# An attention loop in another order, its hand-over to the feed-forward layer a block sooner, and a norm moved from VectorE to ScalarE

## The reference

```python
x = x + attn_a(layernorm(x))   # 2 heads of 64, rotary positions on half of each head, softmax over 256 keys
x = x + ffn(layernorm(x))      # 128 -> 512, gate; 512 -> 512, gelu; 512 -> 512, gelu; 512 -> 128
x = x + attn_b(layernorm(x))   # 16 heads of 8, causal softmax
x = x + ffn(layernorm(x))      # the same weights again
```

## Time and profile before

| | |
|---|---|
| median of 3 runs | 768.71 us (766.55 to 768.84) |
| the profiled execution's own time | 768.21 us |
| its span in the profile | 766.4 us |
| TensorE busy | 685.7 us, 89% |
| VectorE, ScalarE, GpSimd busy | 484.8, 454.9 and 431.0 us |
| granted TensorE clock, mean | 0.977 |

### The profile page before, as it was taken

How to read it: one execution, slowest core, us unless ns; L and a number is a source line. 1 busy time by engine, 2 the same in 40 slices (tenths; PEclk the granted TensorE clock), 3 DMA queues, 4 the chain that set the end, 5 groups by cost and what they waited for, 6 DMA issues and landing times.

```text
span 766.4 us, 13977 instructions
## 1 busy us (share of the span) xinstructions
PE 685.7 (89%) x4706; PEld 472.0 (62%) x4706; DVE 484.8 (63%) x957; ACT 454.9 (59%) x801; POOL 431.0 (56%) x444
## 2 busy tenths in 40 slices
PE   3789896799999999999999999999878899999996
PEld 1455555477787777665555555555445777777784
DVE  6668885567555586456767767766658356675510
ACT  2677774555665565445656566666665555556663
POOL 4455441377867776433444544543555677777763
PEclk9999998899999999999999999999999999999998
DMA  6110320000000003531645654645111000000000
GB/s 182 39 38 20 62 27 2 0 1 1 0 1 0 0 0 99 177 111 43 209 147 177 239 169 156 229 140 180 57 63 41 16 15 15 14 0 15 15 15 27
DMA packets 33028, 52.47 MB, mean 68 GB/s; under 512 B 4560, under 2 KB 9680, under 8 KB 32976
## 3 DMA queue, kind: packets, MB, share of 16 engines
q1 hardware_dynamic: 32784, 51.53, 21.3%
q10 hardware_dynamic: 192, 0.26, 0.1%
HBM read 27.15 MB, written 24.38 MB: 67 GB/s over the span
## 4 chain that ended last, share of the span: by engine, by line
PE 48%; DVE 13%; POOL 13%; issue 12%; ACT 8%; DMA 5%; ACTq 1%; POOLq 1%; DVEq 0%; SPq 0%
PE banks L220 44%; POOL f_h_lo L1122 5%; POOL f_g_lo L1129 5%; ACT b_prob L1448 2%; DMA b_o_dram<-b_o 2%; DVE xn L182 2%; DVE a_mx L645 2%; PE banks L212 2%; ACT a_prob L548 1%; DMA b_den<-b_o_dram 1%; DVE a_prob L657 1%; DVE f_hidden L1072 1%; DVE a_straight L630 1%; PE banks L957 1%; DVE f_gate L1068 1%
## 5 line engine op out<-in xcount | busy, mean ns | idle before, releaser
L1129 POOL TENSOR_TENSOR f_g_lo<-f_gelu,f_g_hi 128x512 fp32r<-128x512 f32 x128 | 167.9, 1316 | 68.8 <-ACT f_g_hi L1024 68.5
L1023 ACT ACTIVATE f_gelu<-banks,cols 128x512 f32<-128x512 f32 x128 | 88.2, 689 | 141.9 <-PE banks L220 139.3
L220 PE MATMUL banks<-f_g_hi,whi 128*128 128x512 f32 x320 | 132.7, 415 | 15.1 <-POOL f_g_lo L1129 15.1
L1534 DVE TENSOR_REDUCE b_segment_max<-banks 128x6 f32<-128x768 f32 x128 | 116.2, 949 | 45.0 <-PE banks L220 44.6
L1644 POOL TENSOR_SCALAR_AFFINE_SELECT b_prob<-b_prob 128x512 f32<-128x512 f32 x128 | 81.7, 641 | 111.6 <-ACT b_prob L1448 111.4
L1448 ACT ACTIVATE b_prob<-banks 128x768 f32<-128x768 f32 x128 | 102.6, 809 | 63.4 <-PE banks L220 55.0
L220 PE MATMUL banks<-f_g_lo,whi 128*128 128x512 f32 x320 | 128.1, 400 | 0.0
L1122 POOL TENSOR_TENSOR f_h_lo<-f_hidden,f_h_hi 128x512 fp32r<-128x512 f32 x60 | 77.5, 1292 | 58.7 <-DVE f_h_hi L1075 58.7
L220 PE MATMUL banks<-f_h_hi,whi 128*128 128x512 f32 x256 | 104.4, 408 | 3.2 <-POOL f_h_lo L1122 2.7
L220 PE MATMUL banks<-f_h_lo,whi 128*128 128x512 f32 x256 | 102.1, 399 | 0.0
L1024 ACT ACTIVATE f_g_hi<-banks,cols 128x512 fp32r<-128x512 f32 x128 | 87.1, 680 | 0.0
(11 more groups left out here) (124 smaller groups left out, 1052.1 us busy)
## 6 DMA issues: line engine op xcount, KB each, us to landing
f_h_hi<-b_q_dram SPq DMA_DIRECT2D x16, 512.0 KB, 4.0
f_h_lo<-b_k_dram SPq DMA_DIRECT2D x16, 512.0 KB, 5.0
b_o_dram<-b_o SPq DMA_DIRECT2D x8, 1024.0 KB, 4.3
b_q_dram<-b_q_hi SPq DMA_DIRECT2D x16, 256.0 KB, 3.2
b_k_dram<-b_k_hi SPq DMA_DIRECT2D x16, 256.0 KB, 3.3
w_stage<-in_wF SPq DMA_DIRECT2D x8, 352.0 KB, 3.2
b_q_dram<-b_q_lo SPq DMA_DIRECT2D x8, 256.0 KB, 3.4
b_k_dram<-b_k_lo SPq DMA_DIRECT2D x8, 256.0 KB, 3.8
```

The lines of the kernel that those rows point to most:

```text
L220: return nc.tensor.matmul(out, lhsT, rhs, start=start, stop=stop)
L1023: nc.scalar.activation(gf[c % 2][:, :], z_bank[c % 2], ACT.Gelu, scale=scale).then_inc(s_gf, 1)
L1129: nc.gpsimd.tensor_tensor(lo[:, c, :], gf[c % 2][:, :], hi[:, c, :].bitcast(F32), ALU.subtract).then_inc(s_glo[c % 2], 1)
L1534: nc.vector.reduce_max(seg[:, g, s, 2 * p:2 * p + 2, :], first_pass[:, 2 * p:2 * p + 2, 0:3 * P].rearrange("p b (c k) -> p b c k", c=3), A ...
```

## The change

It reorders the lists of the first attention, moves its last steps against the first steps of the feed-forward layer, and moves the feed-forward norm. The core of the diff:

```diff
             def pe_body(pe, b, before, one, two):
...
+                pe_scores(pe, b, 1)
                 if one:
                     pe_proj(pe, n1, "k")
-                pe_scores(pe, b, 1)
+                for h in (1, 0):
+                    pe_probT(pe, b, 0, h)
                 if one:
                     pe_proj(pe, n1, "kr")
-                for h in range(HA):
-                    pe_probT(pe, b, 0, h)
-                if before:
-                    pe_out(pe, b.after(-1))
                 pe_pv(pe, b, 0)
                 if one:
                     pe_proj(pe, n1, "v")
+                if before:
+                    pe_out(pe, b.after(-1))
+                if one:
+                    pe_scores(pe, n1, 0)
                 if two:
                     pe_T(pe, n2)
-                if one:
-                    pe_scores(pe, n1, 0)
-                for h in (1, 0):
+                else:
+                    pe.wait_ge(s_tu, 2 * BLOCKS)
+                    nxt["pe_T"](pe, FIRST_BLOCK)
+                for h in (0, 1):
                     pe_probT(pe, b, 1, h)
                 if two:
+                    pe_proj(pe, n2, "qr")
                     pe_proj(pe, n2, "q")
-                    pe_proj(pe, n2, "qr")
+                else:
+                    pe.wait_ge(s_vr, BLOCKS)
+                    ffn["pe_total"](pe)
                 pe_pv(pe, b, 1)
...
             def dve_body(dve, b, before, one, two):
...
                 dve_inverse(dve, b, 0)
                 if two:
                     norm.dve_stats(dve, n2)
+                else:
+                    nxt["norm"].dve_stats(dve, FIRST_BLOCK)
                 dve_normalise(dve, b, 0)
+                dve_max(dve, b, 1)
+                if two:
+                    norm.dve_shift(dve, n2)
+                dve_negate(dve, b, 1)
                 if one:
                     dve_rope(dve, n1, "k")
-                dve_max(dve, b, 1)
-                if one:
                     dve_rope(dve, n1, "kr")
-                if two:
-                    norm.dve_shift(dve, n2)
-                if before:
-                    dve_update(dve, b.after(-1))
                 dve_inverse(dve, b, 1)
+                if not two:
+                    norm.dve_free(dve)
+                    nxt["norm"].dve_apply(dve, FIRST_BLOCK, True)
                 if one:
                     dve_v(dve, n1)
                 dve_normalise(dve, b, 1)
+                if before:
+                    dve_update(dve, b.after(-1))
...
             def pool_body(pool, b, before, one, two):
-                nc.gpsimd.tensor_tensor(xblk(b.t), xblk(b.t), row4("bo"), ALU.add).then_inc(s_bo, 1)
                 if two:
                     norm.pool(pool, b.after(2))
+                else:
+                    link["next"]["norm"].pool(pool, FIRST_BLOCK)
+                nc.gpsimd.tensor_tensor(xblk(b.t), xblk(b.t), row4("bo"), ALU.add).then_inc(s_bo, 1)
...
                 for c in range(KC):
                     act_gelu(act, b, True, c)
+                    if two and c < 2:
+                        norm.act_tiles(act, n2, range(2 * c, 2 * c + 2))
                     if two and c == 2:
                         act_xhi(act, n2)
...
-                    if two and c == 2:
-                        norm.dve_apply(dve, n2, False)
                 if before:
                     dve_down(dve, b.after(-1))
+                if two:
+                    norm.dve_shift(dve, n2)
...
-                    if two and c == 0:
-                        norm.pool(pool, b.after(2))
                     if nxt:
                         nxt["pool_front"](pool, b, "first", c)
+                if two:
+                    norm.pool(pool, b.after(2))
                 for c in range(KC):
                     pool_glo(pool, b, True, c)
```

More of the change, by code:

```diff
@@ L192, in act_apply, with act_tiles @@
             def act_apply(self, act, b):
+                self.act_tiles(act, b, range(TILES))
+            def act_tiles(self, act, b, which):
                 t = b.t
-                act.wait_ge(self.shift, t - 1)
-                act.wait_ge(self.read, t)
-                for s in range(TILES):
+                if which[0] == 0:
+                    act.wait_ge(self.shift, t - 1)
+                    act.wait_ge(self.read, t)
+                for s in which:
                     nc.scalar.activation(xn[:, s, :], X[:, bass.ds(TILES * t + s, 1), :], ACT.Identity,
@@ L473, in pe_body @@
                 n1, n2 = b.after(1), b.after(2)
+                nxt = link["next"]
+                pe_scores(pe, b, 1)
                 if one:
                     pe_proj(pe, n1, "k")
-                pe_scores(pe, b, 1)
+                for h in (1, 0):
+                    pe_probT(pe, b, 0, h)
                 if one:
                     pe_proj(pe, n1, "kr")
-                for h in range(HA):
-                    pe_probT(pe, b, 0, h)
-                if before:
-                    pe_out(pe, b.after(-1))
                 pe_pv(pe, b, 0)
@@ L510, in pe_program @@
                 pe_scores(pe, LAST_BLOCK, 1)
-                pe.wait_ge(s_vr, BLOCKS)
-                ffn["pe_total"](pe)
+                for h in (1, 0):
+                    pe_probT(pe, LAST_BLOCK, 0, h)
+                pe_out(pe, LAST_BLOCK.after(-1))
             def pe_last(pe, parts):
                 nxt = link["next"]
-                pe_out(pe, LAST_BLOCK.after(-1))
-                for h in range(HA):
-                    pe_probT(pe, LAST_BLOCK, 0, h)
-                pe.wait_ge(s_tu, 2 * BLOCKS)
-                nxt["pe_T"](pe, FIRST_BLOCK)
                 pe_pv(pe, LAST_BLOCK, 0)
@@ L524, in pe_last @@
                 nxt["pe_gate"](pe, FIRST_BLOCK, 0, parts)
-                for h in (1, 0):
+                pe.wait_ge(s_ex, UNITS * BLOCKS)
+                nxt["pe_gate"](pe, FIRST_BLOCK, 1, parts)
+                for h in (0, 1):
                     pe_probT(pe, LAST_BLOCK, 1, h)
                 nxt["pe_T"](pe, SECOND_BLOCK)
-                pe.wait_ge(s_ex, UNITS * BLOCKS)
-                nxt["pe_gate"](pe, FIRST_BLOCK, 1, parts)
+                nxt["pe_gate"](pe, FIRST_BLOCK, 2, parts)
                 pe_pv(pe, LAST_BLOCK, 1)
-                for c in range(2, KC):
-                    nxt["pe_gate"](pe, FIRST_BLOCK, c, parts)
+                nxt["pe_gate"](pe, FIRST_BLOCK, 3, parts)
             def pe_tail(pe, at, c):
@@ L573, in act_body @@
                 n1, n2 = b.after(1), b.after(2)
+                nxt = link["next"]
                 if two and not is_block(b, 0):
                     ffn["beside"]["act"](act, n2)
+                act_normalise(act, b, 0)
                 if before:
                     act_out(act, b.after(-1))
-                act_normalise(act, b, 0)
-                for h in range(HA):
+                for h in (1, 0):
                     act_probT(act, b, 0, h)
@@ L586, in act_body @@
                     act_xT(act, n2)
-                for h in (1, 0):
+                else:
+                    nxt["act_xhi"](act, FIRST_BLOCK)
+                for h in (0, 1):
                     act_probT(act, b, 1, h)
@@ L603, in act_program @@
                 nxt = link["next"]
+                act_normalise(act, LAST_BLOCK, 0)
                 act_out(act, LAST_BLOCK.after(-1))
-                act_normalise(act, LAST_BLOCK, 0)
-                for h in range(HA):
+                for h in (1, 0):
                     act_probT(act, LAST_BLOCK, 0, h)
                 act_exp(act, LAST_BLOCK, 1)
-                nxt["act_xhi"](act, FIRST_BLOCK)
                 act_normalise(act, LAST_BLOCK, 1)
                 nxt["act_tanh"](act, FIRST_BLOCK, 0)
-                for h in (1, 0):
+                for h in (0, 1):
                     act_probT(act, LAST_BLOCK, 1, h)
@@ L691, in dve_body @@
                 if two:
+                    dve_rope(dve, n2, "qr")
                     dve_rope(dve, n2, "q")
-                    dve_rope(dve, n2, "qr")
+                else:
+                    ffn["dve_flag"](dve)
+                    nxt["dve_xlo"](dve, FIRST_BLOCK)
                 if is_block(b, 0):
@@ L779, in pool_program @@
                 nxt = link["next"]
-                nxt["norm"].pool(pool, b0)
                 nc.gpsimd.tensor_tensor(xblk(LAST), xblk(LAST), row4("bo"), ALU.add).then_inc(s_bo, 1)
@@ L1676, in pool_front @@
                 if is_block(b, LAST - 2) and (at, c) == ("second", 1):
+                    pool.wait_ge(link["prev"]["norm"].xn, TILES * BLOCKS)
                     norm.pool(pool, FIRST_BLOCK)
```

13 lines of the change are left out of this document (7 added, 6 removed).

## The result

The changed kernel takes **780.37 us** (median of 4 runs, 778.24 to 782.17) against 767.85 for the one before (766.55 to 768.84): ratio 1.0169, 95% interval 1.0147 to 1.0191. It is slower, by less than 2% but clear of the noise; the forecast was 765.3 with a range of 758 to 773. The profiled span went from 766.4 to 780.0 us, +13.6.

What follows compares the result with a forecast made beforehand. It saw TensorE on 48% of the chain, otherwise waiting for other engines, nearly level with VectorE in attention. Terms -7.4 - 1.4 + 7.0 + 1.6 - 3.0 = -3.2 us against 768.21 gave 765.0, stated as 765.3, range 758 to 773.

Steps and rivals of the forecast that it cites:

- Feed-forward, blocks 1 to 5: Ten blocks over both layers: old wait goes, new 1.45 us wait for ScalarE's tiles comes, 0.70 us each, +7.0 us.
- The shift is at 17.7, ScalarE's first tile at 18.0: Feed-forward block: times in us from block start, following POOL's rstd at 17.6, leading to the 1.45 us tile wait.
- The sign that the prediction had set itself: Feed-forward blocks: forecast is wrong if TensorE's wait for ScalarE's tiles is under 0.5 or over 2 us.
- The first rival: Feed-forward norm chain: one more POOL operation or held VectorE cast costs ten blocks 1.25 us each, about 778 us; chance 0.14.
- Behind the 2.15 us gap it was 1.00: Feed-forward gaps: clock could fall, but stayed at 1.00 in the four microseconds after one old gap; costed at nothing.
- Attention loop: Start to block 6's maximum: periods shrink from 13.96 to 12.7 us, block 0's period gives 1.7, together -7.4 us.
- the third rival: Attention loop: VectorE behind wlo, or POOL's rstd before the negative maximum, costs 0.7 a period, about 769 us; chance 0.17.
- TensorE to 12.54: Attention loop: TensorE's period without its 1.42 us wait, 13.96 - 1.42, nearly level with VectorE's 12.5.
- Hand-over: Block 6's maximum to the first feed-forward block's last low part: 34.3 us where 35.7 stood, -1.4 us.
- Blocks 0: First feed-forward block of each layer: +1.6 us in the first layer, -3.0 in the second, with tile waits of 1.9.
- the old slow stretch: Second layer's block 0, behind the b_oTn wait: a projection took 1.89 us; 1.7 counted as gained there.
- The last step of the sum: Whole kernel: from 765.0 us to 765.3, since the median of the runs is 0.5 above the profiled execution.

Runs made afterwards that it cites:

- the feed-forward part alone: Kernel before with only the feed-forward norm moved to the second half and its tiles on ScalarE; attention and hand-over unchanged: 789.30 us (1.0284).

## Why the prediction was wrong

**Feed-forward, blocks 1 to 5: the step that failed** is "The shift is at 17.7, ScalarE's first tile at 18.0". POOL's count was right to a tenth: `rstd` ends 259.84 - 242.26 = 17.6 us in the block. But the shift was priced at next to nothing, and it takes 1.25: the first tile is at 19.0 and TensorE waits 2.26 where 1.45 was forecast. The old wait for the last low part did go, as said. Without the stretches of low clock the ten blocks cost 16.7 us where the sum has 7.0. With the hold gone and all else as it was (the kernel in which POOL lets the shift pass), the five blocks of the first layer take 115.68 us for 112.75 before: 5.9 us for ten, near the 7.0. The sign that the prediction had set itself, a wait of over 2 us, came: 2.08 to 2.39 in these blocks.

I had the right rule in hand and used half of it. The timeline shows the shift ending with the low part that began before it. The Trainium skill, SBUF — State Buffer, section "Who interferes with whom", which the prediction cites for VectorE's fast modes alone, also says that a VectorE instruction with two SBUF inputs contends with a GpSimd instruction that reads SBUF, and one with a single input outside those modes doesn't. The traces agree with both: 1.25 us against 0.16 for the two-input shift beside and without the low part, 0.58 for the four one-input ones beside it. (Both agree if 128x1 is outside the fast modes; no run tests that by itself. The runs show who is held and for how long; that what holds it is a port, no run here shows.) The prediction applied it to the normalisations, where 1.9 us was forecast and 2.02 came, and passed over the small operations because the row of before has them at 0.15 us. That row was taken where POOL was not in the way. Nor was there a conflict between the rule and the old row of 1.25 us beside `wlo`: that pair came 0.84 us after `wlo` had begun and ended 0.42 behind its end, so it had only the rest of it to wait for.

**The first rival was the mechanism**: "one more collision in the norm's chain", 1.25 us a block, about 778 us. It had 0.14. Its argument against was "I have counted the collisions that the lists give". The count left out the one that is no accident: POOL's next instruction is behind `rstd` in its own queue, and the shift can't start before VectorE knows of `rstd`. So POOL begins first every time, 18 of 18: by 0.06 to 0.07 us in the feed-forward layers, by 0.08 to 0.18 in the attention loop, where the shift also stands behind VectorE's maximum.

**The clock** was the other miss. "Behind the 2.15 us gap it was 1.00" generalised from a single wait, with another in the earlier trace rows of 2.10 that a slow projection follows. The changed kernel and the feed-forward part alone have 24 waits for tiles, of 2.08 to 2.55 us; in seven of them the clock is low within the next four microseconds. By comparison with the undisturbed blocks of the first layer (24.37, 24.22, 23.91) that cost 1.55 us in the first layer and 3.4 in the second, less 1.0 that the kernel before paid in its own block 1 of the second (23.57 for 22.56): 16.7 + 4.9 - 1.0 = 20.6, the sum of the two lines of the table, +9.9 and +10.7.

**Attention loop**: -5.0 for -7.4. The TensorE gap ahead of the transposition went and the second normalisation is 2.02, as said; but the third rival's mechanism was there in part, POOL beside the shift in front of the negative maximum (by the bias add, not by `rstd`). It cost 0.9 a period (13.13 to 12.2). That is more than the 0.45 between forecast and result, as "TensorE to 12.54" was wrong the other way: freed by the wait in front of the bias add, TensorE is busy throughout a period of 12.20 (window of that kernel, columns as above):

```profile
67.66:79.86 12.20, 12.20 (x77) 1.00 0.16 45
```

The same for a period of the kernel before:

```profile
73.25:87.18 13.93, 12.51 (x78) 1.00 0.21 55
```

The profile has TensorE busy for 12.51 us in the kernel before as well, with as many matmul records (78 and 77), so the subtraction of the one wait read the rows rightly; but the 12.54 was no floor for the same work. Where the 0.3 us lay is open (the ends of matmuls are modelled in these records).

**Hand-over**: -2.7 for -1.4. The branch comes 15.0 us behind block 6's maximum (14.3 forecast), TensorE goes on at 18.6 (19.2), the last low part is done at 142.9 (near 142). The stop was 3.58, not 4.9. In the kernel before VectorE wrote the flag only when TensorE had already run dry, 0.7 us into the 5.08. Block 7's first scores on TensorE and the flag there, and the scores and the end of the stop in the changed kernel with the one-input shift:

```profile
123.44 1.14 PE L220 MATMUL banks<-a_kT,a_qT 64*128 64x256 f32 x8 [0.73 <-ACT a_prob L548]
125.24 0.14 DVE L857 CAST f_lo_anywhere<-banks 1x1 int32<-1x1 f32 x1
```
```profile
121.19 1.62 PE L230 MATMUL banks<-a_kT,a_qT 64*128 64x256 f32 x8 [0.89 <-ACT a_prob L562]
...
127.79 1.29 PE L230 MATMUL banks<-a_probT,a_v 128*64 128x256 f32 x8 [1.94 <-issue]
```

The rows show that it is the end of the stop that hardly moves, not its length. TensorE goes on 6.33 us behind these scores in the kernel before and 6.72 in the changed one, though 1.25 us of work stands between the scores and the stop in the one and 3.14 in the other. In the kernel with the one-input shift that work took 4.66 (the clock was at 0.68 and 0.50 beside it) and the stop was 1.94: 6.60 again. So work that is put ahead of the branch is in part hidden by the stop, where the forecast set the whole 4.9 behind it. What fixes the end was not tested.

**Blocks 0**: in the first layer +2.5 for +1.6, the tiles' wait 2.51 for 1.9. In the second 0.0 for -3.0. The wait for `b_oTn` went, as forecast, but the tiles' wait is 2.53 for 1.9, and the clock is at 0.50 for two microseconds behind it and at 0.77 for the next two (4.49 us from the transposition to block 1's start; 3.28 where the clock stayed up, with the one-input shift). The wait for the last low part gave 0.6 (2.15 to 1.57), not 1.1. And of the 1.7 counted for the old slow stretch, 1.0 lies behind block 1's start, in the table's next line (it is the 1.0 named under the clock). The longer wait, the clock (1.2), the 0.5 and the 1.0 make up the 3.0, within 0.3.

**Block 6 to the second layer**: -1.9 for 0. Of this 0.7 is block 6 itself, 28.76 us before and 28.09 after; it is 28.1 in every kernel here with the tiles on ScalarE and 28.8 to 29.0 in those with the tiles on VectorE. The rest lies in the second attention and is no gain of the change: from block 7's start to the second layer the other kernels took 258.2 to 262.6, the changed one 260.4.

**The last step of the sum** has a slip: 765.0 and 0.5 are 765.5, not 765.3.

## What to carry to other kernels

When VectorE waits for a result of GpSimd and GpSimd goes straight on to a long operation, VectorE's next operation that needs the shared port is held until that one ends, however small it is. Price it at what is left of GpSimd's next instruction (all of it, if VectorE was only waiting for the result), not at its own, and remove it by having GpSimd wait for the short one, or by one-input forms that are not held themselves (here 128x1). Taking one hold away shows which operation is held next (here the negative maximum), so read the profile again and not only the time. A chain that is moved to a later place should be laid against the moment at which its end is asked for: here one operation earlier on POOL was worth more than the whole of the wait that the move removed.

## What the runs showed of the hardware

An operation of 128x4 elements can take 1.25 us, eight times its 0.15, by nothing but what GpSimd does beside it. Of VectorE's small `tensor_scalar` operations, those on 128x1 ran beside GpSimd's (0.58 us for four), and the one on 128x4 was held (0.72 for the negative maximum, and 1.00 in block 6 of the changed kernel, for 0.15 to 0.17). Whether the shape makes the difference was not tested by itself: the two differ in their scalar operands as well.

TensorE's clock did not fall by the length of a wait alone: of twelve waits for tiles in the changed kernel four have a low clock behind them, and 2.34 us was followed by a fall at 189.76 and by none at 239.89. With the one-input shift none of twelve (1.42 to 1.87 us) was followed by one in the execution that was traced. Its ten times spread from 763.0 to 771.1; the mean clock was 0.986 in the shortest and 0.978 in the longest, but 0.986 also in one of 768.05, so the clock explains the spread at most in part.

The stop for the branch, TensorE idle by "issue", was 5.08 to 5.25 us in the three kernels with the old hand-over and 1.94 to 3.65 in the ten with the new one. Its end came 6.25 to 6.79 us behind the start of block 7's first scores in all thirteen, whether 1.2, 3.1 or 4.7 us of work stood between. Why there is open.
